# An order for each engine, dense products in five PSUM banks, weights in five parts, and two of a unit's eight mask seeds as products on the tensor engine

## What is computed

```python
xn = layernorm(x)
for i in range(4):                       # encoder, the larger part
    h = layer_norm(e, ln1_w[i], ln1_b[i])
    q, k, v = split(h @ Wi[i].T + bi[i])
    s = q @ k.T / sqrt(8) + alibi + causal_mask
    e = e + softmax(s) @ v @ Wo[i].T + bo[i]
    h = layer_norm(e, ln2_w[i], ln2_b[i])
    e = e + gelu(h @ W1[i].T + b1[i]) @ W2[i].T + b2[i]
out = x + layer_norm(e, final_w, final_b) + experts(xn)
```

## Time and profile before

| | us |
|---|---|
| median of 3 runs | 1640.66 (1640.59 to 1646.0) |
| the profiled execution | 1640.9 |
| its span | 1639.1 |
| busy: PE, PEld | 1421.8, 946.2 |
| busy: ACT, DVE, POOL | 1223.2, 1131.8, 614.3 |

### The profile page before, as it was taken

The page is one execution under the profiler, slowest core; times in us unless marked ns, Lnnn a source line. Parts: engine busy times, 40 slices in busy tenths (PEclk is TensorE's granted clock), DMA queues, the critical chain, the costliest instruction groups (busy, mean ns, idle before and its releaser), DMA issues.

```text
span 1639.1 us, 38563 instructions
## 1 busy us (share of the span) xinstructions
PE 1421.8 (87%) x10720; PEld 946.2 (58%) x10720; DVE 1131.8 (69%) x2851; ACT 1223.2 (75%) x2165; POOL 614.3 (37%) x1052
## 2 busy tenths in 40 slices
PE   0677787568999999999999999999999989999995
PEld 0445554335666666666666666666666656666653
DVE  6567676347777777677677766777776767777762
ACT  3233333238999898898999888999888988888884
POOL 5232222123333343333333333334333345555443
PEclk9999888779999999999999999999999999999997
DMA  3332333045444444444444445444444444444430
GB/s 107 100 114 89 107 92 101 24 122 149 121 124 127 117 116 126 134 129 119 120 129 119 122 121 133 129 119 121 127 119 123 129 128 125 124 125 125 123 90 10
DMA packets 104789, 187.60 MB, mean 114 GB/s; under 512 B 19912, under 2 KB 70728, under 8 KB 104720
## 3 DMA queue, kind: packets, MB, share of 16 engines
q1 hardware_dynamic: 89904, 150.45, 33.3%
q0 software_dynamic: 14848, 36.72, 8.3%
HBM read 120.87 MB, written 65.01 MB: 113 GB/s over the span
## 4 chain that ended last, share of the span: by engine, by line
PE 53%; DVE 17%; issue 14%; DMA 9%; POOL 2%; DVEq 1%; ACT 1%; SPq 1%; POOLq 0%; ACTq 0%
PE pvp L979 11%; PE exp_ps L956 7%; DVE negm L698 6%; PE mxp L923 6%; PE dense L1009 6%; PE dense L1018 5%; PE dense L868 5%; DMA blocks<-split_L 4%; PE mxp L927 4%; DVE xn L666 3%; PE dense L896 2%; PE dense L997 2%; DVE ost L744 2%; PE mxp L868 2%; DMA blocks<-negt 2%
## 5 line engine op out<-in xcount | busy, mean ns | idle before, releaser
L831 ACT ACTIVATE probs<-exp_ps 128x512 f32<-128x512 f32 x896 | 525.0, 593 | 289.1 <-PE exp_ps L956 286.4
L698 DVE TENSOR_REDUCE negm<-mxp 128x2 f32<-128x512 f32 x896 | 569.2, 683 | 90.3 <-PE mxp L927 72.6
L956 PE MATMUL exp_ps<-qbd_l,kst_l 128*128 128x512 f32 x768 | 368.5, 495 | 8.3 <-issue 4.3
L923 PE MATMUL mxp<-blocks,qst 104*128 104x512 f32 x768 | 325.5, 453 | 34.5 <-DMA blocks<-split_L 19.7
L855 ACT ACTIVATE exp_ps<-masktf 128x512 f32<-128x512 f32 x513 | 308.8, 602 | 22.6 <-DVE rest L766 6.5
L927 PE MATMUL mxp<-maskb,identb 128*128 128x256 bf16 (+1 forms) x768 | 247.6, 322 | 0.0
L498 POOL TENSOR_SCALAR veps<-mv 128x2 f32<-128x2 f32 x144 | 31.7, 220 | 560.9 <-DVE mv L657 557.2
L923 PEld LDWEIGHTS mxp<-blocks,qst 104*128 104x128 f32 x768 | 149.0, 194 | 84.2 <-DVE negm L698 37.0
L979 PE MATMUL pvp<-probs,vst_l 128*32 128x256 f32 (+1 forms) x4096 | 194.5, 330 | 0.6 <-ACT probs L831 0.6
L744 DVE COPY ost<-pvp 128x512 f32<-128x512 f32 x80 | 55.3, 692 | 201.6 <-PE pvp L979 201.6
L956 PEld LDWEIGHTS exp_ps<-qbd_l,kst_l 128*128 128x128 f32 x768 | 144.4, 195 | 40.8 <-issue 31.3
(11 more groups left out here) (95 smaller groups left out, 2006.6 us busy)
## 6 DMA issues: line engine op xcount, KB each, us to landing
split_L<-hi SPq DMA_DIRECT2D x256, 128.0 KB, 2.1
qst<-split_L SPq DMA_DIRECT2D x64, 384.0 KB
kst_l<-split_L SPq DMA_DIRECT2D x64, 384.0 KB
qbd_l<-split_L SPq DMA_DIRECT2D x256, 96.0 KB
split_L<-lo POOLq DMA_DIRECT2D x128, 128.0 KB, 2.1
blocks<-split_L SPq DMA_DIRECT2D x128, 96.0 KB
blocks<-split_L POOLq DMA_DIRECT2D x128, 96.0 KB, 4.4
split_F<-hi SPq DMA_DIRECT2D x64, 128.0 KB, 2.1
```

The costliest lines, as they stand in the source:

```text
L698: dve.tensor_reduce(heads[:, g, first:first + count], mxp[:, (plan.max_chunks * g + ch) % 3, :].rearrange("p (h t) -> p h t", h=count), AX ...
L831: act.activation(probs[:, g[0], ch, :], exp_ps[:, (plan.exp_chunks * g[0] + ch) % 2, :], ACT.Exp, scale=plan.scale).then_inc(q.b_exp, 1)
L923: pe.matmul(mxp[:, bank, :], qst[0:BIAS_END, g[0], qt * P:(qt + 1) * P], kbd[0:BIAS_END, first:first + count, g[0], 0:keys], start=True, s ...
L956: pe.matmul(exp_ps[:, bank, :], kst[plan.name][:, s, g[0], kt * P:(kt + 1) * P], rhs, start=not on_diagonal, stop=True, skip_group_check=T ...
```

## The change

The order. `slot_steps` of the encoder is a new list, in which each engine's part of a step has a name of its own, so each engine gets an order of its own. Steps that were fused come apart: `rstd`, `rstd2`, `xb`, `xb2`, `lo`, `smaxp` are GpSimd's, `y`, `gelu` ScalarE's, `hi` VectorE's, and `hi>`, `row>`, `smax>`, `stack>` are SyncE's (storing `hi`, the row of maxima, the loads for the maxima and for the exps). f1 and f2 are in two halves. The first norm and its transpose are one unit further ahead (s+3), so the encoder has a further round at its start.

```diff
         if self.causal:
...
-                exps[0:2] + at("ot", s - 1) + at("ln", s + 2) + at("ot+", s - 1) + at("v v+", s + 1) + at("xn", s + 2)
-                + at("f2 f2+", s - 2) + at("at at+", s - 1)
-                + exps[2:3] + maxes[0:2] + at("xt", s + 2)
-                + exps[3:4] + maxes[2:4] + at("xt+", s + 2) + at("op", s - 1) + at("stack+", s + 1)
-                + exps[4:5] + maxes[4:5] + at("op+", s - 1) + at("qk", s + 2)
-                + exps[5:6] + maxes[5:7] + at("qk+", s + 2)
-                + exps[6:7] + maxes[7:9] + at("xn2", s - 1) + end
-                + exps[7:8] + maxes[9:11]
-                + exps[8:9] + maxes[11:12]
-                + exps[9:10] + at("xt2 xt2+", s - 1) + values[0:2] + end2
-                + exps[10:11] + at("negt negt+", s + 1) + at("stack_max+", s + 2)
-                + exps[11:12] + at("f1 f1+", s - 1) + values[2:4] + at("pv+", s) + store)
+                at("w=o w=w1", s - 1) + at("hi> xt", s + 2) + at("row>", s + 1)
+                + part("exp", s, 0) + at("ot", s - 1)
+                + part("exp", s, 1) + at("xb", s - 1) + part("f2", s - 2, 0) + at("v+", s + 1) + at("w:v", s + 2)
+                + at("at+ at", s - 1)
+                + part("exp", s, 2) + at("ot+", s - 1)
+                + part("exp", s, 3) + at("op", s - 1) + at("ln", s + 3) + at("op+", s - 1) + part("f2", s - 2, 1)
+                + at("w:w2", s - 1) + at("rstd", s + 3)
+                + part("exp", s, 4) + at("f2+", s - 2) + end + part("max", s + 1, 0, 1) + at("rstd2", s - 1)
+                + at("smax>", s + 2)
+                + part("exp", s, 5) + at("xn2", s - 1) + at("w=v y", s + 2) + part("max", s + 1, 2)
+                + end2 + at("qk", s + 2) + at("w:qk", s + 3)
+                + part("exp", s, 6) + at("hi", s + 2) + part("pv", s, 0) + part("max", s + 1, 3)
+                + part("exp", s, 7) + at("xt2 w=w2", s - 1) + part("max", s + 1, 4, 5)
+                + part("exp", s, 8) + part("max", s + 1, 6, 7) + at("lo", s + 2)
+                + part("exp", s, 9) + part("max", s + 1, 8) + part("pv", s, 1) + at("xt2+", s - 1)
+                + part("max", s + 1, 9)
+                + part("exp", s, 10) + at("w=qk", s + 3) + part("max", s + 1, 10)
+                + part("exp", s, 11) + part("max", s + 1, 11) + part("f1", s - 1, 0) + part("gelu", s - 1, 0, 1)
+                + at("xb2", s - 1) + at("w:o", s) + at("negt+ negt", s + 1) + at("xn", s + 3) + part("f1", s - 1, 1)
+                + at("w:w1", s) + part("pv", s, 2) + at("xt+", s + 3) + part("pv", s, 3) + at("smaxp", s + 2)
+                + at("pv+", s) + at("stack> v", s + 2) + store)
```

```diff
+EXPERT = Plan("F", 8, False, False, BATCH // 2, {
+    "xt": 1, "qk": 1, "v": 0, "at": 1, "op": 0, "negt": 1, "ot": 4})
+ENCODER = Plan("L", 16, True, True, LAYERS * BATCH // 2, {
+    "xt": 2, "qk": 0, "v": 0, "at": 1, "op": 0, "xt2": 0, "negt": 4, "f2": 4, "ot": 1, "f1": (0, 1)})
```

```diff
+SEEDER = {0: "PE", 2: "PE", 3: "ACT", 5: "ACT", 6: "ACT", 8: "ACT", 9: "ACT", 11: "ACT"}
...
+                        last = pe.matmul(o, kst[plan.name][:, s, g, kt * P:(kt + 1) * P], rhs,
+                                         start=seeder not in ("ACT", "DVE"), stop=True, skip_group_check=True)
+                        if seeder == "PE":
+                            last = pe.matmul(o, identb[:, :], masktb.rearrange("p h t -> p (h t)"), start=False, stop=True,
+                                             skip_group_check=True)
```

```diff
+WEIGHTS = {
+    "qk": ("a", A_Q, A_V), "v": ("a", A_V, A_COLS),
+    "o": ("c", C_O, C_W1), "w1": ("c", C_W1, C_W2), "w2": ("c", C_W2, C_COLS)}
...
+                    if step[0:2] in ("w:", "w="):
+                        part = step[2:]
+                        begins = not inner and (2 * k + off) % BATCH == 0
+                        of = layer + (2 * k + off) // BATCH if begins else None
+                        if step[0:2] == "w:" and begins and not (isinstance(of, int) and of == 0):
+                            last_use(part, of)
+                            load_weights(part, of)
+                        if step[0:2] == "w=" and s == 0:
+                            if begins:
+                                sp.wait_ge(q.w[part], 16 * (of + 1))
+                                settle(sp, passed_sp)
+                            sp.sem_inc(q.w_ok[part], 1)
...
                     elif step == "op":
-                        if plan.causal:
-                            pe.wait_ge(q.wc_ok, u + 1)
+                        if plan.causal and s == 0:
+                            pe.wait_ge(q.w_ok["o"], r + 1)
```

More of the change, by code:

```diff
@@ L79, in at, with part @@
             return [(name, unit) for name in names.split()]
-        exps = [("exp", s, *divmod(k, self.exp_chunks)) for k in range(self.exp_chunks * GROUPS)]
-        maxes = [("max", s + 1, *divmod(k, self.max_chunks)) for k in range(self.max_chunks * GROUPS)]
-        values = [("pv", s, g) for g in range(GROUPS)]
+        def part(name, unit, *numbers):
+            return [(name, unit, k) for k in numbers]
         if self.causal:
@@ L284, in build @@
         mxp = ps("mxp", [P, 3, 512])
+        bank = dense + [mxp[:, k, :] for k in range(3)]
         exp_ps = ps("exp_ps", [P, 2, 512])
@@ L503, in steps @@
                 q = S[plan.name]
-                for step, u, s, r, g, _ in plan.steps(n, last_layer):
-                    if step == "ln":
+                for step, u, s, r, _, _ in plan.steps(n, last_layer):
+                    if step == "rstd":
                         inverse_deviation(q, "A", u, s)
+                    elif step == "rstd2":
+                        inverse_deviation(q, "C", u, s)
                     elif step == "end":
@@ L714, in steps @@
                 q = S[plan.name]
[L715 removed]
+                for step, u, s, r, k, _ in plan.steps(n, last_layer):
                     bt = u % BATCH if plan.causal else u
@@ L811, in steps @@
                 q = S[plan.name]
-                for step, u, s, r, g, _ in plan.steps(n):
+                chunks = plan.exp_chunks * GROUPS
+                for step, u, s, r, k, _ in plan.steps(n):
                     if step == "xt+":
@@ L859, in _ @@
             act.wait_ge(S["F"].c_done, BATCH)
-            seed(0)
-            rounds_of(act, ENCODER, lambda n: steps(ENCODER, n))
+            for k in range(2):
+                if SEEDER.get(k) == "ACT":
+                    seed(k)
+            encoder_rounds(act, lambda n, last_layer=False: steps(ENCODER, n))
         @block.tensor
```

459 lines of the change are left out of this document (242 added, 217 removed).

## The result

The changed kernel takes 1794.7 us, the median of four runs (1793.54 to 1796.8), against 1643.19 for the kernel before in the same comparison: a ratio of 1.092, with the 95% interval 1.090 to 1.095. The forecast was 1710, with a range from 1620 to 1755. The sign was right; the size was not, and the time lies 40 us above the range.

A forecast was written before the change was run, and what follows sets the result against it. Three engines were near their limit, so the order's chains of waits were taken to bound the kernel. The span 1639.1 + 19 (48 steps) + 50 (last layer) = 1708, with 1.8 around it 1710 us; range 1620 to 1755.

The forecast's parts named there:

- +19 us for 48 steps: Encoder steps ahead of the last layer: slot pairs average 20.05 us against 19.65, +0.4 each (+9 to +31 in all).
- SyncE's queue: Every second slot, an even unit's op count stands behind stack>, which waits for smax> to land: N+9.0 to N+9.9.
- The second kind of slot: Slots whose op belongs to an even unit and waits for SyncE's count: 20.7 to 21.6 us, 21.15 taken.
- inside the same 9 us: An even unit's v also waits for its count, N+3.15 against N+2.5, hidden within op's wait for its count.
- the rival in which this wait vanishes: SyncE's wait is hidden, all slots take 18.95 us and the last layer 22.7: 1641 us; chance 0.12.
- The last layer: The final norm (end) ahead of rstd2 delays xn2: slots 22.7 and 25.5, mean 24.1 against 20.33, +50 us.
- The first kind of slot: Slots whose op belongs to an odd unit: VectorE's chain 18.7, tensor engine's sum with waits 18.9; 18.95 us taken.
- the tensor engine's sum of 17.5 us a unit: Its products priced from the chain of waits: 17.0 us a unit before, plus 0.5 for two mask products.
- the rival of 1531 us: The order beats the counted chains; the tensor engine sets 17.9 us a unit, 18.5 in the last layer; chance 0.13.
- Layer changes: Three steps before were some 4 us longer waiting for weights; loading in five parts mostly removes these 12 us.
- The seeds: Two of eight leave ScalarE, 1.2 us a unit; mask products add 0.5 on the tensor engine; little gained.
- Slower still: Rival: smax>'s landing takes 7 us or more, or hi> is late behind it: above 1755 us; chance 0.10.

The follow-up runs named there:

- experiment 1: The changed kernel with SyncE's counts w=o and w=w1 raised ahead of stack> instead of behind it; 1756.06 us, ratio 1.066.
- Experiment 2: The kernel of experiment 1 with both parts of the final norm later in the list, the first behind xn2; 1708.54 us, ratio 1.038.
- experiment 10: The changed kernel with one edit alone, the query and key products ahead of the third maximum on the tensor engine; 1790.36 us, ratio 1.087.
- the fastest kernel: The kernel of experiment 9, fastest of all the kernels run; 1597.31 us, ratio 0.970.
- experiment 9: The kernel of Experiment 4 with the query and key products ahead of the third maximum on the tensor engine; 1597.31 us, ratio 0.970.
- Experiment 4: The kernel of Experiment 2 with xt before the last value group, and loads and counts of v and qk ahead of row>; 1614.35 us, ratio 0.979.
- Experiment 5: The kernel before, in its old order, with the masks of exp products 0 and 2 added by the tensor engine; 1650.92 us, ratio 1.002.
- experiment 12: The changed kernel with each of a unit's two mask products issued twice; 1797.09 us, ratio 1.093.
- experiment 6: The kernel of Experiment 4 with all eight seeds on ScalarE, none on the tensor engine; 1648.23 us, ratio 0.999.
- experiment 11: The fastest kernel with each of a unit's two mask products issued twice; 1619.26 us, ratio 0.984.

## Why the prediction was right in sign and wrong in size

The forecast was +19 us for 48 steps and +50 for the last layer. It came out as +92 and +55.

*SyncE's queue: right.* The mechanism, its place and every second slot are as forecast. In the slot shown `negt`'s product starts at 924.16 and the even unit's `op` at 933.70, 9.5 us later; the forecast took 9.0 to 9.9. The second kind of slot is 21.9 in a steady stretch, forecast 21.15 with an upper end of 21.6; the rest is the step behind `op`, below. One step of the reasoning was not right: `v`'s wait for its own count was to lie "inside the same 9 us". It does while the other wait is there, but with that one gone (experiment 1) `v`'s 0.87 us stay, and the second kind falls to 20.87 and not to 20.20. The Trainium skill's fit of 2.0 us and the bytes at 436 GB/s (DMA: Bandwidth & Descriptors, Anatomy of one DMA), which it gives for one transfer on GpSimd's path, was the rule of the rival in which this wait vanishes. For several loads from SyncE's queue the trace disagrees here too, with 5.25 us from the first issue to the end of the wait for the landing.

*The last layer: right.* Forecast 22.7 and 25.5 in turn, mean 24.1; measured 22.9 in three steps and 24.0 to 24.4 in the three others of that kind, and 25.3 to 26.0 in the second, mean 24.60. In the slot shown above xn2 starts 6.1 us after the add, forecast 6.0. Experiment 2 gives back 47.5 us by undoing nothing else, up to 15 of them by way of the clock, which the forecast did not have.

*The first kind of slot: the step that failed.* Forecast 18.95 us, measured 20.20; 24 of them make 30 us. From `negt` to the next slot it took 3.17 us (forecast 3.0), from there to `op` 4.60 (4.5), and from `op` to `negt` 12.43, where the forecast's chain had 11.2 (0.7 to the add and 10.5 behind it; the chain gave 18.7, and 18.95 was taken). So nearly all of the miss is behind `op`, and it is in both kinds of slot: from the add to `negt` 11.5 and 11.3 us, forecast 10.5. There I let VectorE set the time, "without a gap", with the tensor engine's sum just equal (11.3 for the products behind `op`, at the forecast's prices). In the trace VectorE has gaps. The one ahead of `hi` is ended by ScalarE, those behind it by the tensor engine, which in the same stretch has next to no idle time (last row, columns of the earlier trace rows):

```profile
959.69 0.43 DVE L720 CAST hi<-y 128x512 fp32r<-128x512 f32 x1 [0.33 <-ACT y L879]
...
964.59 1.89 DVE L745 TENSOR_REDUCE negm<-mxp 128x4 f32<-128x512 f32 x3 [0.39 <-PE mxp L982]
967.12 0.41 DVE L784 CAST negt<-mxp 16x256 fp32r<-16x256 f32 x1 [0.65 <-PE mxp L926]
...
954.18:966.61 12.43, 12.37 (x86) 7.69 (x87) 9.98 (x21) 10.18 (x19) 4.61 (x8) 1.00 0.43 127
```

The term that was too small is the tensor engine's sum of 17.5 us a unit. Of the 1.2 us behind `op`, 0.3 are what experiment 10 took away; 12.0 to 12.1 is the least that any order run with this work between `op` and `negt` shows. In the fastest kernel a unit is 18.9, with next to no idle time to see, and `op` to `negt` is 12.15 us (888.99 to 901.14). The price of 0.23 us for an exp product, a maximum and a wide mask each was the error: three in turn take 0.79 in the rows of experiment 9, not 0.69. From start to start through one slot of that kernel, the twelve exp products, the twelve maxima and all their masks come to 9.1 us and not to 7.9, and f1 to 2.0 and not to 1.7. It is the products that were priced too low, 0.31 to 0.36 each on average; a mask's start is followed by the next after 0.07 on average, less than its price. The chain of waits has a product's start to the next *step of the chain*, and that is not always the next product. At these rates the rival of 1531 us, with its 17.9 a unit, was out of reach.

*Layer changes: wrong.* The forecast let 12 us go away because the weights come in five parts. Instead the three changes take 144.2 us for their six steps (24.38, 22.21, 25.57, 24.36, 24.87, 22.84), 18 more than three pairs of the steady lengths. The step that failed: I asked whether `v`'s count is late in a steady slot ("inside the same 9 us") and not when the *loads* are issued at a change. That of `v` stands behind `row>` in the same queue, that of `qk` behind the issues of `smax>`, and so their landings come on top: 2.16 us for `v`, and 4.96 us of ScalarE for `qk`, of which the forecast says nothing. It is the very rule that I had applied to `w=o`. Experiment 4 moves the loads and counts and takes the bulge in these steps away. Its 44 us are more than the 18, since it also takes waits for the counts off ScalarE's `xt+` (1.03 us) and off `v` (0.4 us) in every second slot.

*The seeds: right that they buy little here.* The forecast put them at nothing much, since two chains stood within 0.3 us of each other. Experiment 5 finds no gain in the old order, experiment 12 that the tensor engine's part costs nothing in the changed kernel, and experiment 6 34 us of gain once the order no longer stands in the way. The Trainium skill's advice to go by weight-load busy share (Trainium Kernel Development and Optimization, Performance Expectations; it names matmul flops against the peak beside it, which was not worked out here) misleads: the share is 65% in the fastest kernel, whose step experiment 11 lengthened with two short products.

*The chances.* "Slower still" had 0.10 and named a landing after 7 us or a late `hi>`. The time came out there, but by neither. The case that I left out was that several small terms err in one direction. The 85 us that were missing are: 24 steady pairs at 42.1 instead of 40.1, 48; the three layer changes, 18; the first layer, whose second kind of slot takes up to 23.7, 7; the last layer and the last two units, 5; and 6 at both ends, which the forecast took as unchanged.

What stays open: why the first layer's slots are longer than the second's with the same order; what lowered the clock in the last layer of experiment 10; and whether work taken off the tensor engine between `op` and `negt` would shorten the step, which no run tests.

## What to carry to other kernels

In an in-order queue a step that only raises a count, or only asks for a load, is as late as the longest wait ahead of it: for each step that is moved, write down what stands ahead of it in *that* queue, in steady state and once more at each change of phase. Take an engine's need per unit from starts to starts in a stretch without waits, summed over all its products, and not from steps of a chain; and to find out whether an engine is on the path of a stretch, give it a little more work in that stretch and look whether the step grows. More than one engine can pass that test. Offloading work from an engine pays only once its own chain is the late one, so mend the order first and judge the offload after.

## What the hardware showed that was not expected

After some waits of the tensor engine of one to two microseconds, products that follow take longer and the granted clock of the stretch falls. Stretches of the changed kernel (columns of the earlier trace rows), then two of its output products in the last layer:

```profile
1016.00:1024.00 8.00, 4.76 (x37) 3.26 (x30) 2.78 (x11) 4.31 (x8) 0.75 (x2) 1.00 0.53 142
1024.00:1030.00 6.00, 5.70 (x25) 4.42 (x25) 3.33 (x11) 2.88 (x6) 2.71 (x6) 0.72 0.39 99
1030.00:1040.00 10.00, 9.99 (x88) 5.96 (x91) 8.17 (x15) 9.01 (x17) 5.38 (x9) 1.00 0.28 95
...
1458.51 1.22 PE L1056 MATMUL dense<-wc_l,attnt 128*128 128x128 f32 x4 [1.75 <-SPq L484]
...
1556.98 1.22 PE L1056 MATMUL dense<-wc_l,attnt 128*128 128x128 f32 x4 [1.14 <-SPq L484]
```

At a layer change the engine is busy 4.8 of 8 us at the full clock, and in the 6 us after that the clock is 0.72, some of it at the lower of its two levels. Then it is full again. In steady slots, where the wait is 0.73, the product takes its 0.71. The length of the wait alone does not decide it: in the kernel before, the output product of the earlier trace rows takes its 0.71 after a wait of 1.55, and the clock stays full there, although the engine is busy 4.7 of 6.5 us:

```profile
1003.50:1010.00 6.50, 4.72 (x24) 3.04 (x23) 4.19 (x11) 4.58 (x10) 1.95 (x5) 1.00 0.58 162
1010.00:1020.00 10.00, 9.39 (x96) 5.91 (x96) 5.91 (x13) 8.65 (x16) 4.42 (x7) 1.00 0.53 145
```

So a wait can be paid for a second time shortly after it, and undoing it can give back more than the wait. Experiments 2 and 4 gave twice what was expected of them, and the clock can be only a part of that: some 15 of 25 us at most in experiment 2, and at most 10 of 22 in experiment 4, where the mean granted clock of the 48 steps goes from 0.99 of 965 us to 1.00. Neither share was tested by itself.
